# Vision-tower attention: even slots of 100 maxima, two blocks ahead, and 17 bursts of two column-tiled groups per half in place of 25 of one or two

## The chip, the cores and the metric

The kernel runs on one core of a Trainium2 chip. The metric is the device time of one execution in microseconds (us). All four compute engines are used: TensorE (PE in the profile), VectorE (DVE), ScalarE (ACT) and GpSimd (POOL); SyncE (SP) issues nearly all DMAs.

## The reference

```python
h = _L0_tok_ref(x, ...)                                   # windows of 4x4, 8 heads, on 4 images of 56x56x256
h = h + _L0_attn_ref(_layernorm(h), qkv_w, qkv_b, proj_w, proj_b, rpb_table)
h = h + _L0_ffn_ref(_layernorm(h), ...)                   # half of the tokens by a gate, up, gelu, down

def _L0_attn_ref(x, qkv_w, qkv_b, proj_w, proj_b, rpb_table):
    qkv = (x @ qkv_w + qkv_b).reshape(Bw, Nw, 3, nh, dh)  # Bw = 4 images, Nw = 3136 tokens, nh = 8, dh = 32
    q, k, v = (qkv[:, :, 0], qkv[:, :, 1], qkv[:, :, 2])
    attn = jnp.einsum('bnhd,bmhd->bhnm', q * scale, k)
    bias = jnp.transpose(rpb_table[rel_idx], (2, 0, 1))
    attn = jax.nn.softmax(attn + bias[None], axis=-1)
    out = jnp.einsum('bhnm,bmhd->bnhd', attn, v).reshape(Bw, Nw, Cd)
    return out @ proj_w + proj_b
```

The change touches only the middle one, the full attention over the 3136 tokens of each image; its projection is made in a later stage.

## The kernel before, in words

Four stages follow each other: `setup_tables`, `windows_and_qkv`, `full_attention`, `gated_ffn`. Only `full_attention` (from L865) is changed.

**Tiles.** The work is cut into 8 phases (4 images, 2 groups of 4 heads), each phase into 7 halves of `CH` = 448 queries: 56 halves in all. Keys are cut into `KT` = 25 tiles, the first of 64 keys, the others of 128. A half makes 100 scores, one for each key tile and head (`score`, L1130): a product of 97 rows, keys on the output's partitions, 448 queries along it, into one of three banks of `ps_s`. The 97 rows are three stacked parts of 32 (high and low parts of key and query) and a row of ones against a row of shifts. ScalarE takes the exponential of each score from PSUM into `prob`, which has `SLOTS` = 5 places of one key tile and four heads (L1264 to L1279); before it writes place t it waits for the `weigh` and the sum that read the tile five before.

**Shifts and fills.** Softmax needs a shift for each query, its greatest score. It is found a half ahead: for the next half's blocks of `BLK` = 128 queries TensorE makes the products with queries on the partitions (`fill`, L1173), for 4 heads and 7 pieces of 448 keys each, into one of `MB` = 3 banks of `ps_m`; VectorE reduces each to a maximum (`take`, L1288, L1302), reduces the seven of a block for two heads to a negative shift (L1307), TensorE transposes the shifts of four blocks (a "turn", L1184), VectorE copies them (L1297) and SyncE moves them into row 96 of the query tile (`shifts`, L1026). A fill may start only when the reduce of the entry three before it is done (L1179). `max_entries` (L835) lists a phase's 714 entries, 700 maxima and 14 turns, in order, and cuts them into seven slots by `SPILLS`, of 108, 98, 102, 98, 102, 98 and 108 entries; slot s+1 is worked on during half s. The 7 groups of blocks have 4, 3, 4, 3, 4, 3 and 4 blocks. The first block of a group is read from the end of the query tile of the half before, which is `AHEAD` = 5 blocks wide; the others from the group's own tile. The last half has no entries.

**Order on TensorE** (`half`, L1225). After each of the 100 scores come as many entries as keep step with their number, which with 102 is one, and two after scores 49 and 99, and then the burst of that place, if there is one. A burst holds one or two column-tiled groups. A group is four products of 128 rows and 32 output columns, one for each head and each into its own 32 partitions, of 448 queries, in full fp32; each is two instructions, so a group is eight. `weigh` (L1149) multiplies one key tile's `prob` by the values into `ps_o`; `total` (L1161) sums over the partitions, either `prob` of the first tile or one of eight sums over several key tiles that GpSimd adds up (`SUM_TILES`, L1111), into `ps_d`. 25 weighs and 9 totals make 34 groups a half. `weigh` of tile t stands after score 4(t+1)+3, `total` k with the one of them that is 15 scores behind its last tile's first score (L1212 to L1223). So there are 25 bursts, every fourth score, nine of them of two groups. Weigh 24 and totals 7 and 8 fall into the next half.

**Order on VectorE** (`half`, L1326). It takes the entries in their order; before entry `KEEP_AT` = 4 it copies `ps_o` of the half before (`keep_out`, waits for its last weigh), and before entries at 28, 36, ... 84 hundredths of the slot it makes one of 8 reciprocals of `den` (L1320).

**ScalarE** copies `ps_d` to `den` after tile 3 (`keep_den`, L1259). **GpSimd** makes 16 additions a half and one product out x den (`normalize`, L1096), after the addition of tile 21. **SyncE** issues in this order each half: queries of the next half, part of the next phase's keys, the first pair's shift rows, the store of the half before (waits for `normalize`), the second pair's shift rows (L1037 to L1055).

Of the kernel before, what the change touches and what calls it, by code (L numbers as in the profile page):

```python
# [6 lines left out]
ALU = mybir.AluOpType  # L7
ACT = mybir.ActivationFunctionType
AX = mybir.AxisListType
F32 = mybir.dt.float32  # L10
# [9 lines left out]
N = SIDE * SIDE  # L20
NH = 8
DH = C // NH
# [802 lines left out]
AHEAD = 5 * BLK  # L825
# [4 lines left out]
SPILLS = [10, 22, 10, 22, 10, 22, 16]  # L830
# [4 lines left out]
def max_entries():  # L835

    entries, ends = [], []
    for s, blocks in enumerate(GROUP_BLOCKS):
        entries += [("max", s, blocks[0], j, c) for j in range(HG) for c in range(PER_IMAGE)]
        for p in range(2):
            entries += [("max", s, r, j, c) for r in blocks[1:] for j in (2 * p, 2 * p + 1) for c in range(PER_IMAGE)]
            entries.append(("turn", s, p))
    for e in [e for e in entries if e[0] == "turn"]:
        at = entries.index(e)  # L850
        entries.remove(e)
        entries.insert(min(len(entries), at + TURN_AFTER), e)
    maxes, need = 0, [MAX_EACH * (blocks[-1] + 1) + spill for blocks, spill in zip(GROUP_BLOCKS, SPILLS)]
    need[-1] -= SPILLS[-1]
    for n, e in enumerate(entries):
        maxes += e[0] == "max"
        if maxes == need[len(ends)] and (n + 1 == len(entries) or entries[n + 1][0] == "max"):
            ends.append(n + 1)
    begins = [SPILLS[-1]] + ends[:-1]
    slots = [[(e, 0) for e in range(a, z)] for a, z in zip(begins, ends)]  # L860
    slots[-1] += [(e, 1) for e in range(SPILLS[-1])]
    return entries, slots


def full_attention(nc, d):  # L865

    with ExitStack() as ctx:
# [15 lines left out]
        ident = sb("ident3", [128, 128])  # L883
# [107 lines left out]
        def _(sp):  # L991
# [23 lines left out]
            def load_ahead(x):  # L1015

                for row, part in ((0, 0), (DH, 0), (2 * DH, 1)):
                    sp.dma_start(queries[1 - x.v][row:row + DH, :, 4 * BLK:5 * BLK].bitcast(F32),
                                 d.q[x.g, part, :, bass.ds(x.b * N, BLK)].rearrange("(j d) n -> d j n", j=HG)
                                 ).then_inc(ahead_in, 16)  # L1020
# [5 lines left out]
            def shifts(x, p):  # L1026

                sp.wait_ge(m_used, ONE + ENTRIES * x.p + entry_of_turn(x.s, p) + 1)
                for j in range(2):
                    sp.dma_start(queries[x.v][STACK:STACK + 1, 2 * p + j, 0:4 * BLK].bitcast(F32),  # L1030
                                 shift_rows[p][j:8:2, :].bitcast(F32)).then_inc(shift_in[p], 16)
# [51 lines left out]
        def _(pool):  # L1083
            nc.gpsimd.memset(ident[:, :], 0.0).then_inc(id_zero, 1)
            pool.wait_ge(id_zero, ONE + 1)
            nc.gpsimd.affine_select(out=ident[:, :], in_=ident[:, :], compare_op=ALU.not_equal, fill=1.0, base=0,
                                    pattern=[[-1, 128]], channel_multiplier=1).then_inc(id_set, 1)
            pool.wait_ge(id_set, ONE + 1)
            nc.gpsimd.tensor_copy(ident_r[:, :], ident[:, :]).then_inc(idr_set, 1)
# [37 lines left out]
        def _(pe):  # L1127
# [45 lines left out]
            def fill(y, e, next_phase):  # L1173
# [6 lines left out]
                if kind == "turn":  # L1180
                    pair, = what
                    pe.wait_ge(shift_ready, ONE + 2 * PER_IMAGE * p + 2 * group + pair + 1)
                    base = TILE_BLOCK[group]
                    nc.tensor.transpose(ps_m[0:8, e % MB, 0:BLK],  # L1184
                                        shift[:, pair, base:base + 4, :].rearrange("q b j -> q (b j)"),
                                        ident[:, :]).then_inc(m_ready, 1)
                    return
# [3 lines left out]
                ahead = r == GROUP_BLOCKS[group][0] and not very_first  # L1191
# [4 lines left out]
                if j % 2 == 0 and c == 0 and r == (0 if very_first else GROUP_BLOCKS[group][1]):  # L1196
                    pe.wait_ge(q_in[v][j // 2], ONE + 24 * (y.h - y.v) + 48)
                tile = queries[1 - v if ahead else v]
                at = 4 * BLK if ahead else BLK * (r - TILE_BLOCK[group])
# [11 lines left out]

            bursts = {i: [] for i in range(TILES)}  # L1212
            for t in range(KT):
                i = HG * (t + 1) + 3
                bursts[i % TILES].append((weigh, t, i >= TILES))
            bursts[HG * 4 + 3].append((total, 0, False))
            for k, tiles in enumerate(SUM_TILES):
                i = HG * tiles[-1] + 15
                while not bursts[i % TILES]:
                    i += 1  # L1220
                bursts[i % TILES].append((total, k + 1, i >= TILES))
            for i in bursts:
                bursts[i].sort(key=lambda item: not item[2])  # L1223
# [27 lines left out]
            weigh(end, KT - 1)  # L1251
            for i in range(TILES):
                for what, k, of_before in bursts[i]:
                    if of_before and what is total:
                        total(end, k)

        @block.scalar
        def _(act):
# [5 lines left out]
            def half(x):  # L1264
                for t in range(KT):
# [14 lines left out]
                    if t == 3 and x.has_before:  # L1280
                        keep_den(x.h - 1)
# [5 lines left out]
        def _(dve):  # L1287
# [35 lines left out]
            KEEP_AT = 4  # L1323
# [738 lines left out]
```

## Time and profile before

| | us |
|---|---|
| median of 3 runs | 6077.67 |
| lowest, highest | 6074.65, 6080.56 |
| the profiled execution's own time | 6058.31 |
| its span, first to last instruction | 6056.4 |
| PE busy | 5790.5 |
| POOL busy | 4386.0 |
| DVE busy | 4380.1 |
| ACT busy | 3273.6 |

The profile is of one execution. A matmul's row begins when it or its weight load begins, and its end is modelled, so matmuls overlap in it: prices on PE are read from start to start. PEld is the weight load; it is the weight load that carries a matmul's waits. A row of the timeline may merge several instructions of one kind (x4): its duration is from the first one's start to the last one's end. Busy times are the union of the intervals.

### The profile page before, as it was taken

The page shows a single profiled execution, that of the slowest core. Times are in us where ns is not written, and L with a number is a line of the kernel's source. Part 1 is how long each engine was busy: PE and PEld are TensorE (multiplying, and loading weights), DVE is VectorE, ACT ScalarE, POOL GpSimd, SP SyncE. Part 2 cuts the span into 40 slices and gives each one's busy share as a digit, 9 for nine tenths or more (in the row PEclk, how much of TensorE's full clock was granted, in tenths as well). Part 3 has the DMA queues.
Part 4 walks back from the last instruction along what each step waited for, and adds up shares of the span by engine and source line. Part 5 has one row for each costly group of instructions (what it writes and reads, how often), then busy time and mean ns, then how long its engine had stood idle before and what let it go on. Part 6 is the DMA issues. An engine that isn't in the chain of part 4 may idle for free. (4 is left out here: it accounts for less than half of the span.)

```text
span 6056.4 us, 121185 instructions
## 1 busy us (share of the span) xinstructions
PE 5790.5 (96%) x37698; PEld 3429.1 (57%) x37698; DVE 4380.1 (72%) x8484; ACT 3273.6 (54%) x6740; POOL 4386.0 (72%) x1475
## 2 busy tenths in 40 slices
PE   5999998999999999999999999999999999984899
PEld 4777776555555555555555555555555555533566
DVE  4777776777877777777777777777777777736540
ACT  3555454266666666666666666666666666652222
POOL 2444444588888888888888888888888888875453
PEclk9999999799999999999999999999999999997899
DMA  2323223211011111101101110111111000015442
GB/s 73 100 93 105 95 98 112 62 35 37 16 37 33 28 25 37 36 17 37 33 27 25 37 36 17 37 33 27 25 37 36 16 17 17 15 31 160 119 98 44
DMA packets 197572, 297.79 MB, mean 49 GB/s; under 512 B 38038, under 2 KB 162334, under 8 KB 193998
## 3 DMA queue, kind: packets, MB, share of 16 engines
q1 hardware_dynamic: 181958, 269.42, 15.8%
q0 software_dynamic: 12432, 19.38, 1.6%
q8 instruction: 274, 4.49, 0.3%
q10 hardware_dynamic: 2680, 2.63, 0.1%
q14 instruction: 228, 1.87, 0.1%
HBM read 167.63 MB, written 124.50 MB: 48 GB/s over the span
## 5 line engine op out<-in xcount | busy, mean ns | idle before, releaser
L1302 DVE TENSOR_REDUCE tops<-ps_m 128x1 f32<-128x448 f32 (+1 forms) x5600 | 3116.7, 616 | 899.3 <-PE ps_m L1205 863.5
L1278 ACT ACTIVATE prob<-ps_s 128x448 f32<-128x448 f32 (+1 forms) x5600 | 2613.1, 548 | 1739.3 <-PE ps_s L1141 1696.8
L1111 POOL TENSOR_TENSOR tile_sum<-prob 128x1792 f32<-128x1792 f32 x448 | 1803.2, 4025 | 647.2 <-ACT prob L1278 646.8
L1141 PE MATMUL ps_s<-queries,keys 97*128 97x448 f32 (+1 forms) x5600 | 2197.3, 397 | 12.5 <-ACT prob L1278 7.6
L1205 PE MATMUL ps_m<-keys,queries 96*128 96x448 f32 (+1 forms) x5600 | 2090.1, 380 | 28.1 <-DMA keys<-k_parts 25.6
L1111 POOL TENSOR_TENSOR tile_sum<-tile_sum,prob 128x1792 f32<-128x1792 f32 x448 | 1808.0, 4036 | 31.8
L1141 PEld LDWEIGHTS ps_s<-queries,keys 97*128 97x128 f32 (+1 forms) x5600 | 1041.4, 187 | 1152.9 <-ACT prob L1278 661.4
L1157 PE MATMUL ps_o<-prob,values 128*32 128x448 f32 x11200 | 1341.8, 551 | 3.0 <-ACT prob L1278 1.2
L1205 PEld LDWEIGHTS ps_m<-keys,queries 96*128 96x128 f32 (+1 forms) x5600 | 1061.2, 190 | 234.1 <-DVE tops L1302 89.5
L1157 PEld LDWEIGHTS ps_o<-prob,values 128*32 128x32 f32 x11200 | 226.5, 108 | 379.4 <-issue 245.0
L1169 PE MATMUL ps_d<-tile_sum,ones 128*32 128x448 f32 x3584 | 420.9, 541 | 3.3 <-POOL tile_sum L1111 3.3
L331 POOL TENSOR_TENSOR logit<-logit,top 112x896 f32<-112x896 f32 x112 | 190.5, 1701 | 237.3 <-DVE top L602 237.3
L612 DVE RECIPROCAL rden<-sums 128x224 f32<-128x224 f32 x112 | 173.6, 1550 | 123.9 <-ACT sums L751 123.9
L391 PE MATMUL ps_q<-xT,w_qkv 128*128 128x224 f32 x896 | 203.2, 371 | 50.7 <-DMA bias_proj<-in_b_proj 50.7
L1169 PEld LDWEIGHTS ps_d<-tile_sum,ones 128*32 128x32 f32 x3584 | 110.7, 110 | 211.4 <-issue 206.5
L1320 DVE RECIPROCAL den<-den 128x56 f32<-128x56 f32 x448 | 217.5, 488 | 14.5 <-ACT den L1262 14.5
L342 POOL TENSOR_TENSOR lo<-full,hi 128x448 fp32r<-128x448 f32 x112 | 127.2, 1136 | 116.8 <-DVE hi L658 116.8
L337 POOL TENSOR_TENSOR rstd<-veps,minus_half 112x4 f32<-112x4 f32 x28 | 33.8, 1208 | 240.2 <-DVE veps L647 240.2
L391 PEld LDWEIGHTS ps_q<-xT,w_qkv 128*128 128x128 f32 x896 | 163.6, 193 | 63.4 <-DMA bias_proj<-in_b_proj 50.7
L1712 PE MATMUL ps_h<-xT,w_up 128*128 128x512 f32 (+1 forms) x416 | 179.9, 584 | 0.9 <-ACT xT L1776 0.7
L1722 PE MATMUL ps_y<-w_down,hT 128*128 128x256 f32 x784 | 177.1, 381 | 0.0
L739 ACT ACTIVATE prob<-logit 112x896 f32<-112x896 f32 x112 | 106.0, 947 | 123.5 <-POOL logit L331 123.4
(181 smaller groups left out, 4096.3 us busy)
## 6 DMA issues: line engine op xcount, KB each, us to landing
queries<-q_parts SPq DMA_DIRECT2D x288, 160.0 KB, 3.3
keys<-k_parts SPq DMA_DIRECT2D x96, 392.0 KB, 7.1
xT<-in_x SPq DMA_DIRECT2D x56, 224.0 KB, 2.6
hidden_and_bias<-base SPq DMA_DIRECT2D x28, 448.0 KB, 3.1
q_parts<-hi SPq DMA_DIRECT2D x56, 224.0 KB, 1.9
q_parts<-lo SPq DMA_DIRECT2D x56, 224.0 KB, 1.9
k_parts<-hi SPq DMA_DIRECT2D x56, 224.0 KB, 1.9
k_parts<-lo SPq DMA_DIRECT2D x56, 224.0 KB, 1.9
```

The lines of the kernel that those rows point to most:

```text
L331: nc.gpsimd.tensor_tensor(logit[p][:, :, :], logit[p][:, :, :], top[p][:, :].unsqueeze(2).broadcast_to([GROUP, NH, GROUP]), ALU.subtract). ...
L391: mm = nc.tensor.matmul(ps_q[:, bank, k * UNIT:(k + 1) * UNIT], w[:, c, job * 128:(job + 1) * 128], xT[u][:, c, :], start=(c == 0), stop=( ...
L1111: nc.gpsimd.tensor_tensor(tile_sum[k % 2][:, :, :], left, prob[:, t % SLOTS, :, :], ALU.add).then_inc(summed, 1)
L1141: mm = nc.tensor.matmul(o[:, 0:CH], keys[x.u][:, j, at:at + k], queries[x.v][:, j, own:own + CH], start=True, stop=not last, skip_group_ch ...
L1157: mm = nc.tensor.matmul(ps_o[j * DH:(j + 1) * DH, 0:CH], values[x.u][:, t, j * DH:(j + 1) * DH], prob[:, t % SLOTS, j, :], start=(t == 0), ...
L1169: mm = nc.tensor.matmul(ps_d[j * DH:(j + 1) * DH, 0:CH], ones[:, int(k > 0), :], moving, start=(k == 0), stop=(k == SUMS))
L1205: mm = nc.tensor.matmul(o[:, 0:CH], tile[0:STACK, j, at:at + rows], keys[u][0:STACK, j, c * CH:(c + 1) * CH], start=True, stop=not corner, ...
L1278: nc.scalar.activation(prob[0:k, t % SLOTS, j, :], ps_s[0:k, score_bank(x.hm, i), 0:CH], ACT.Exp).then_inc(exp_done, 1)
L1302: nc.vector.tensor_reduce(tops[0:rows, j, r - blocks[0], c:c + 1], ps_m[0:rows, e % MB, 0:CH], AX.X, ALU.max).then_inc(m_used, 1)
L1320: nc.vector.reciprocal(den[:, piece * w:(piece + 1) * w], den[:, piece * w:(piece + 1) * w]).then_inc(recip_done, 1)
L1712: mm = nc.tensor.matmul(ps_h[:, t % 2, 0:w], w_up[:, c, t * 128:(t + 1) * 128], xT[:, c, 0:w], start=(c == 0), stop=(c == CT - 1))
L1722: mm = nc.tensor.matmul(ps_y[:, r // 2, (r % 2) * C:(r % 2 + 1) * C], hT[:, t, r * ROWS:(r + 1) * ROWS], w_down[:, t, :], start=(t == 0), ...
```

## The change

- A group's first two blocks (`MORE` = 2), no longer one, are read from the tile of the half before, so the query tiles are 6 blocks wide (`OWN` + `MORE`) and `load_ahead` brings two blocks.
- `SPILLS` are such that every slot has 100 maxima and 2 turns.
- The bursts are written out: 17 a half, after scores 3, 11, 16, 21, 26, 31, and then every sixth to 97, each of two groups; eight of them hold two weighs, nine a weigh and a total. Weigh 0 stands after score 16 (7 before), total 0 too (19 before); weigh 24 after score 11 of the next half (3 before).
- `KEEP_AT` is 12, and ScalarE's `keep_den` comes after score 13, no longer after score 15.
- The fp32 identity is built in `out[0]` and not kept; the turns use the rounded one.

```diff
--- before.py
+++ after.py
@@ -822,12 +822,13 @@
 
 
 BLK = 128
-AHEAD = 5 * BLK
+OWN, MORE = 4, 2
+AHEAD = (OWN + MORE) * BLK
 PHASES = B * G
 GROUP_BLOCKS = [range(-(-7 * s // 2), -(-7 * (s + 1) // 2)) for s in range(PER_IMAGE)]
 TILE_BLOCK = [7 * s // 2 for s in range(PER_IMAGE)]
 MAX_EACH = HG * PER_IMAGE
-SPILLS = [10, 22, 10, 22, 10, 22, 16]
+SPILLS = [8, 24, 12, 28, 16, 32, 20]
 TURN_AFTER = 3
 SUM_TILES = [(1, 2, 3, 4)] + [(t, t + 1, t + 2) for t in range(5, 23, 3)] + [(23, 24)]
 
@@ -842,9 +843,9 @@
 
     entries, ends = [], []
     for s, blocks in enumerate(GROUP_BLOCKS):
-        entries += [("max", s, blocks[0], j, c) for j in range(HG) for c in range(PER_IMAGE)]
+        entries += [("max", s, r, j, c) for r in blocks[:MORE] for j in range(HG) for c in range(PER_IMAGE)]
         for p in range(2):
-            entries += [("max", s, r, j, c) for r in blocks[1:] for j in (2 * p, 2 * p + 1) for c in range(PER_IMAGE)]
+            entries += [("max", s, r, j, c) for r in blocks[MORE:] for j in (2 * p, 2 * p + 1) for c in range(PER_IMAGE)]
             entries.append(("turn", s, p))
     for e in [e for e in entries if e[0] == "turn"]:
         at = entries.index(e)
@@ -880,7 +881,6 @@
         corner_lo = sb("corner_lo3", [128, HG, BLK], F32R)
         prob = sb("prob3", [128, SLOTS, HG, CH])
         tile_sum = [sb(f"tile_sum{i}", [128, HG, CH]) for i in range(2)]
-        ident = sb("ident3", [128, 128])
         ident_r = sb("ident_r", [128, 128], F32R)
         ones = sb("ones3", [128, 2, DH])
         tops = sb("tops", [BLK, HG, 4, PER_IMAGE])
@@ -1015,8 +1015,8 @@
             def load_ahead(x):
 
                 for row, part in ((0, 0), (DH, 0), (2 * DH, 1)):
-                    sp.dma_start(queries[1 - x.v][row:row + DH, :, 4 * BLK:5 * BLK].bitcast(F32),
-                                 d.q[x.g, part, :, bass.ds(x.b * N, BLK)].rearrange("(j d) n -> d j n", j=HG)
+                    sp.dma_start(queries[1 - x.v][row:row + DH, :, OWN * BLK:AHEAD].bitcast(F32),
+                                 d.q[x.g, part, :, bass.ds(x.b * N, MORE * BLK)].rearrange("(j d) n -> d j n", j=HG)
                                  ).then_inc(ahead_in, 16)
 
             def load_corner(x):
@@ -1027,7 +1027,7 @@
 
                 sp.wait_ge(m_used, ONE + ENTRIES * x.p + entry_of_turn(x.s, p) + 1)
                 for j in range(2):
-                    sp.dma_start(queries[x.v][STACK:STACK + 1, 2 * p + j, 0:4 * BLK].bitcast(F32),
+                    sp.dma_start(queries[x.v][STACK:STACK + 1, 2 * p + j, 0:OWN * BLK].bitcast(F32),
                                  shift_rows[p][j:8:2, :].bitcast(F32)).then_inc(shift_in[p], 16)
 
             def store(x):
@@ -1081,12 +1081,12 @@
 
         @block.gpsimd
         def _(pool):
-            nc.gpsimd.memset(ident[:, :], 0.0).then_inc(id_zero, 1)
+            nc.gpsimd.memset(out[0][:, 0:128], 0.0).then_inc(id_zero, 1)
             pool.wait_ge(id_zero, ONE + 1)
-            nc.gpsimd.affine_select(out=ident[:, :], in_=ident[:, :], compare_op=ALU.not_equal, fill=1.0, base=0,
-                                    pattern=[[-1, 128]], channel_multiplier=1).then_inc(id_set, 1)
+            nc.gpsimd.affine_select(out=out[0][:, 0:128], in_=out[0][:, 0:128], compare_op=ALU.not_equal, fill=1.0,
+                                    base=0, pattern=[[-1, 128]], channel_multiplier=1).then_inc(id_set, 1)
             pool.wait_ge(id_set, ONE + 1)
-            nc.gpsimd.tensor_copy(ident_r[:, :], ident[:, :]).then_inc(idr_set, 1)
+            nc.gpsimd.tensor_copy(ident_r[:, :], out[0][:, 0:128]).then_inc(idr_set, 1)
             pool.wait_ge(idr_set, ONE + 1)
             nc.gpsimd.memset(ones[:, 1, :], 1.0).then_inc(rows_set, 1)
             for u in range(2):
@@ -1183,20 +1183,20 @@
                     base = TILE_BLOCK[group]
                     nc.tensor.transpose(ps_m[0:8, e % MB, 0:BLK],
                                         shift[:, pair, base:base + 4, :].rearrange("q b j -> q (b j)"),
-                                        ident[:, :]).then_inc(m_ready, 1)
+                                        ident_r[:, :].bitcast(F32)).then_inc(m_ready, 1)
                     return
                 r, j, c = what
                 u, v = (y.u + next_phase) % 2, (y.v + group + PER_IMAGE * next_phase - y.s) % 2
                 very_first = isinstance(p, int) and p == 0 and group == 0
-                ahead = r == GROUP_BLOCKS[group][0] and not very_first
+                ahead = r in GROUP_BLOCKS[group][:MORE] and not very_first
                 if group == 0 and r == 0 and c == 0:
                     pe.wait_ge(k_in[u][j], ONE + 48 * (y.b + int(next_phase and y.g == 1) + 1))
                     if j == 0 and not very_first:
                         pe.wait_ge(ahead_in, ONE + 48 * p)
-                if j % 2 == 0 and c == 0 and r == (0 if very_first else GROUP_BLOCKS[group][1]):
+                if j % 2 == 0 and c == 0 and r == (0 if very_first else GROUP_BLOCKS[group][MORE]):
                     pe.wait_ge(q_in[v][j // 2], ONE + 24 * (y.h - y.v) + 48)
                 tile = queries[1 - v if ahead else v]
-                at = 4 * BLK if ahead else BLK * (r - TILE_BLOCK[group])
+                at = BLK * (OWN + r - GROUP_BLOCKS[group][0] if ahead else r - TILE_BLOCK[group])
                 rows = min(BLK, N - BLK * r)
                 corner = r == 0 and c == PER_IMAGE - 1
                 if corner and j == 0:
@@ -1209,18 +1209,22 @@
                                           start=False, stop=True, skip_group_check=True)
                 mm.then_inc(m_ready, 1)
 
+
             bursts = {i: [] for i in range(TILES)}
-            for t in range(KT):
-                i = HG * (t + 1) + 3
-                bursts[i % TILES].append((weigh, t, i >= TILES))
-            bursts[HG * 4 + 3].append((total, 0, False))
-            for k, tiles in enumerate(SUM_TILES):
-                i = HG * tiles[-1] + 15
-                while not bursts[i % TILES]:
-                    i += 1
-                bursts[i % TILES].append((total, k + 1, i >= TILES))
-            for i in bursts:
-                bursts[i].sort(key=lambda item: not item[2])
+
+            def burst(i, *groups):
+                bursts[i % TILES] += [(what, k, i >= TILES) for what, k in groups]
+
+            burst(16, (weigh, 0), (total, 0))
+            burst(21, (weigh, 1), (weigh, 2))
+            burst(26, (weigh, 3), (weigh, 4))
+            for k, tiles in enumerate(SUM_TILES[:6]):
+                i, t = HG * tiles[-1] + 15, 5 + 3 * k
+                burst(i, (total, k + 1), (weigh, t))
+                burst(i + 6, (weigh, t + 1), (weigh, t + 2))
+            burst(TILES + 3, (total, 7), (weigh, 23))
+            burst(TILES + 11, (weigh, 24), (total, 8))
+            assert len(SUM_TILES) == 8 and KT == 25
 
             def half(x):
                 y = after(x)
@@ -1248,11 +1252,10 @@
             pe.wait_ge(rows_set, ONE + 3)
             halves(pe, half)
             end = Half(FIRST_ROUND, HALVES - 1)
-            weigh(end, KT - 1)
             for i in range(TILES):
                 for what, k, of_before in bursts[i]:
-                    if of_before and what is total:
-                        total(end, k)
+                    if of_before:
+                        what(end, k)
 
         @block.scalar
         def _(act):
@@ -1277,8 +1280,8 @@
                         act.wait_ge(s_ready, ONE + x.h * TILES + i + 1)
                         nc.scalar.activation(prob[0:k, t % SLOTS, j, :], ps_s[0:k, score_bank(x.hm, i), 0:CH],
                                              ACT.Exp).then_inc(exp_done, 1)
-                    if t == 3 and x.has_before:
-                        keep_den(x.h - 1)
+                        if t == 3 and j == 1 and x.has_before:
+                            keep_den(x.h - 1)
 
             halves(act, half)
             keep_den(HALVES - 1)
@@ -1320,7 +1323,7 @@
                 nc.vector.reciprocal(den[:, piece * w:(piece + 1) * w],
                                      den[:, piece * w:(piece + 1) * w]).then_inc(recip_done, 1)
 
-            KEEP_AT = 4
+            KEEP_AT = 12
             RECIP_SCORES = [2 * HG * (k + 3) + HG for k in range(RECIPS)]
 
             def half(x):
```

## Rows read from the trace of the kernel before

**Rows 1.** The page: engines' busy time, and the granted clock in 40 slices

```profile
PE 5790.5 (96%) x37698; PEld 3429.1 (57%) x37698; DVE 4380.1 (72%) x8484; ACT 3273.6 (54%) x6740; POOL 4386.0 (72%) x1475
...
PEclk9999999799999999999999999999999999997899
```

**Rows 2.** Windows, the attention stage: stretch, us, busy (count) by engine, clock, DMA

```profile
core 0: us, PE busy (x) PEld busy (x) DVE busy (x) ACT busy (x) POOL busy (x), PEclk, DMA share, GB/s
1140.12:5426.80 4286.68, 4260.91 (x26513) 2320.57 (x26511) 3298.22 (x6196) 2637.06 (x5655) 3668.39 (x951) 1.00 0.11 28
```

**Rows 3.** Windows with the maxima (L1205) alone: four halves, one phase

```profile
2131.94:2211.02 79.08, 39.74 (x106) 20.05 (x106) 1.00 0.06 17
...
1750.91:1826.92 76.01, 36.86 (x100) 18.94 (x100) 1.00 0.16 41
1826.92:1901.65 74.73, 35.31 (x96) 18.17 (x96) 1.00 0.14 33
...
2052.49:2131.94 79.45, 39.01 (x106) 18.55 (x106) 1.00 0.06 16
...
1675.12:2211.02 535.90, 258.64 (x700) 131.02 (x700) 1.00 0.12 30
```

**Rows 4.** Waits from 1400 to 5000 us: total us, times, longest

```profile
PEld ps_m L1205 <- DVE tops L1302: 55.8, 209, 0.4
```

**Rows 5.** Timeline of PE from 2057 us: start us, us, instruction

```profile
2057.78 0.96 PE L1157 MATMUL ps_o<-prob,values 128*32 128x448 f32 x8
2058.67 0.47 PE L1141 MATMUL ps_s<-queries,keys 97*128 97x448 f32 x1
2058.98 0.37 PE L1205 MATMUL ps_m<-keys,queries 96*128 96x448 f32 x1
...
2060.22 0.37 PE L1205 MATMUL ps_m<-keys,queries 96*128 96x448 f32 x1
2060.51 0.96 PE L1169 MATMUL ps_d<-tile_sum,ones 128*32 128x448 f32 x8
...
2062.16 0.47 PE L1141 MATMUL ps_s<-queries,keys 97*128 97x448 f32 x1
```

**Rows 6.** Timeline of all engines from 2061 us

```profile
2062.47 0.58 PE L1205 MATMUL ps_m<-keys,queries 96*128 96x448 f32 x2
...
2062.88 2.75 DVE L1302 TENSOR_REDUCE tops<-ps_m 128x1 f32<-128x448 f32 x5 [1.27 <-PE ps_m L1205]
...
2063.55 0.19 PEld L1205 LDWEIGHTS ps_m<-keys,queries 96*128 96x128 f32 x1 [0.27 <-DVE tops L1302]
...
2063.86 0.36 PE L1141 MATMUL ps_s<-queries,keys 97*128 97x448 f32 x1
...
2064.49 0.96 PE L1157 MATMUL ps_o<-prob,values 128*32 128x448 f32 x8
```

**Rows 7.** Timeline of all engines from 2173 us: a reciprocal between reduces

```profile
2172.65 1.15 DVE L1302 TENSOR_REDUCE tops<-ps_m 128x1 f32<-128x448 f32 x2
...
2173.72 0.49 DVE L1320 RECIPROCAL den<-den 128x56 f32<-128x56 f32 x1
...
2174.12 0.56 DVE L1302 TENSOR_REDUCE tops<-ps_m 128x1 f32<-128x448 f32 x1
...
2174.60 0.26 DVE L1297 CAST shift_rows<-ps_m 8x128 fp32r<-8x128 f32 x1
```

**Rows 8.** Timelines of POOL, SP and PE at a half's end

```profile
2434.65 1.17 POOL L1098 TENSOR_TENSOR out<-out,den 128x448 f32<-128x448 f32 x1
...
2435.99 0.38 SPq L1035 DMA_DIRECT2D attention_out<-out  x1
2436.48 1.23 SPq L1030 DMA_DIRECT2D queries<-shift_rows  x2
...
2439.93 0.42 PE L1141 MATMUL ps_s<-queries,keys 97*64 97x448 f32 x1
```

## The prediction

> **What bounds the kernel now.** I read the page first: TensorE is busy 96% of the span, and its granted clock has the digit 9 in nearly every slice [rows 1]. Then the windows: the attention stage, from its first score to its last group, is 4287 us of the 6056, with PE busy 4261, DVE 3298, ACT 2637, POOL 3668, clock 1.00, the 2.4 GHz level [rows 2]. Per half (56 of them) that is 76.5 us long, DVE 58.9, ACT 47.1, POOL 65.5. So PE sets the pace, and the change touches only this stage.
>
> Next the halves: one with 98 entries (96 maxima in the row, two turns) takes 74.7 us, with 102 entries 76.0, with 108 entries 79.1 and 79.5; a whole phase of seven takes 535.9 [rows 3]. Four entries more cost 1.3 us, but the next six cost 3.2: beyond 102 something else than streaming is paid. The waits name it: the weight load of a maximum waits 55.8 us in 209 cases for DVE's reduce, because ps_m has three banks [rows 4].
>
> The PE timeline gives the prices [rows 5]. Score and maximum alternate 0.207 us apart (2058.98 to 2060.22 is six steps). From a burst's first matmul to the next score a burst of one group takes 0.89, of two 1.64: a group streams 0.75. A run of four pairs and a burst of one is 2060.51 - 57.78 = 2.73 us; less 8 x 0.207 and 0.75, **0.33 us is the fixed price of going to column tiles and back**. Check: a half with 98 entries has 25 x 0.33 + 34 x 0.75 = 33.75, plus 198 x 0.207 = 41.0, together 74.7, as the row says. It has no stall. By the same sum 102 entries give 75.6 and 108 give 76.8: stalls of 0.4, and of 2.3 and 2.6. A phase before has two halves of 102 and two of 108: 5.8 us of stall.
>
> **Step 1, bursts.** 34 groups stay (25 weigh, 9 total); 25 switches become 17. Over 56 halves 8 x 0.33 x 56 = **-148 us**. Eight of the new bursts hold two weighs, one bank for both, which no row shows. Bounds: 1.64 us as with ps_d beside it, or 2 x 0.89 = 1.78 if the second had to begin afresh, which would cost up to 8 x 56 x 0.14 = 63 us; below 1.64 nothing is to be had, as 0.75 per group is streaming. I take 1.64: within a group both passes of a head already go to one bank, and a group into ps_o and one into ps_d last 0.96 alike [rows 5].
>
> **Step 2, even slots.** The entries stay 714 a phase, so PE streams the same; every half gets 102. The 108-entry halves' stalls go. I take all the old stalls out here and put all new ones in below: 7 phases x 5.8 and 0.9 in the last (which has no following phase to fill for) = **-42 us**.
>
> **Step 3, the longer runs between bursts.** This is the step that decides. In a run PE delivers a maximum each 0.414 us, DVE takes 0.53: five reduces in 2.75 us, four steps after one of 0.61 [rows 6]. Three banks and the burst, during which DVE catches up, hide that while a run has four maxima. The run of rows 6 has five, two of them back to back, and shows the rule. First maximum at 2062.47, its reduce 2062.88 (+0.41) to 2063.49; the fourth maximum's weight load starts 2063.55, the next score at 2063.86, so the fourth really began streaming 0.21 before that, 2063.65: 0.16 after the reduce's end. So with F0 = 0, the maximum k may not stream before 0.41 + 0.61 + 0.53 (k - 3) + 0.16 = 1.18 + 0.53 (k - 3). Unhindered it comes at 0.414 k. The excess of the last maximum is the run's stall: five maxima 1.71 - 1.66 = 0.05; six 2.24 - 2.07 = 0.17; eight 3.30 - 2.90 = 0.40; seven in six score steps (two back to back) 2.77 - 2.28 = 0.49. Applied to rows 6 (the fifth at 1.71 instead of 1.45) it gives 0.26; the run lasts 2064.49 - 62.16 = 2.33 against 1.84 and 0.21 for the extra entry, so 0.28.
>
> The new bursts stand after scores 3, 11, 16, 21, 26, 31, then every sixth to 97. One run of eight pairs (4 to 11): 0.40. Four of five pairs: 0.20. From 98 over the border to 3, six scores with seven entries, as each half's hundredth score carries two: 0.49. Eleven of six pairs, of which that of 44 to 49 has seven entries: 10 x 0.17 + 0.49 = 2.2. Sum 3.3.
>
> On top come the reciprocals. One back to back with reduces costs DVE 0.41 (2173.72 to 2174.12) [rows 7]. They are put before entries 28, 36, 44, 53, 61, 69, 77, 85. Those at a run's first entry (44, 69) fall into the burst; those at its fifth or later (36, 61, 85) delay no release that the run still needs; 28 (second of 27 to 31), 53 and 77 (third of six) delay the last release by 0.41 each: 1.2. Together 4.5 us a half; the turns (a small reduce more, but a cast of 0.26 [rows 7] for a reduce of 0.61) about cancel. 55 halves carry entries: 55 x 4.5 = **+248 us**. In the old order runs had four maxima, and a reciprocal delayed only releases behind the next burst. KEEP_AT 12 puts the copy of ps_o (0.6 us) before the first reduce behind burst 11; weigh 24 leads that burst and its 0.96 and the copy end within the 1.64 and the 0.7 until DVE is wanted: nothing.
>
> **Step 4, what else moves.** Weighs come later (0 at 16 instead of 7, 24 at 111 instead of 103), so ScalarE's five prob slots could run short. Tile t needs weigh t-5: tile 5 begins at score 20, weigh 0 is at 16; tile 11 at 44, weigh 6 at 37; always at least three scores of room. keep_den after score 13 has burst 11 before it, and total 0 stands behind weigh 0 in burst 16: 2.1 + 0.75 us for two exponentials and a copy: nothing. POOL needs 65.5 us a half, 12 under the new one, and no total moves nearer its sum than in the old order. Two blocks ahead make the query loads 768 columns wide; DMA is at 0.11 [rows 2], and the first entry that needs the new tile comes at entry 24 to 48 of a half instead of 6: hidden. On SP the shift rows of the second pair are queued behind the store, which waits for POOL's normalize: ends 2435.82, store issued 2435.99, shifts 2436.48 to 2437.71, while the score that needs them comes in the half that begins 2439.93 (the row with 64 keys), at its third [rows 8]. With two bursts instead of four in that stretch (1.5 us less) this room shrinks but stays: nothing, 56 us if not. The prologue does two entries less: -1. The spare identity is gone, no time.
>
> **The sum.** -148 - 42 + 248 - 1 = +57 us against the profiled execution's 6058.3 (span 6056.4): 6115. The median of the runs is 19 above it, so I forecast 6077.7 + 57 = 6135 us, with halves of 41.8 + 31.1 + 4.5 = 77.4 us, all nearly alike.
>
> The trace shows DVE with 77% of the stage [rows 2], so by busy time alone it binds nothing; it binds inside a run. The Trainium skill (TensorEngine Tiling (Array Packing), PSUM Bottleneck) warns that once tiling has sped TensorE up, the copy out of PSUM may become the limit. Taken as a rule for the average, DVE's 59 us a half would lie far below PE's 73 and the change would win; this case's waits [rows 4] side with the warning, but per run.
>
> **Rivals.** *Not slower:* DVE keeps up in the long runs, say because the reduce of the burst's leftover is always done and releases come earlier than the 0.16 that I read from one run. It is decided at (148 + 42 + 1) / 55 = 3.5 us of stall a half; below that the gains win. With no more stall than now (0.7) the time is 6078 - 191 + 39 = 5926; with releases earlier by 0.05 and reciprocals harmless it is 4.5 - 0.7 - 1.2 = 2.6 a half, 6030. For it: DVE is idle a quarter of the time. Against: rows 3, where six entries more cost 3.2 us instead of 1.2. Chance 0.09. *Slower by more:* the shift rows arrive 1 us late in every half, behind normalize and store on SP, 6135 + 56 = 6191; or two weighs in a burst cost 1.78, 6198. For it: 1.5 us less room, no row of such a burst. Against: 2 us are free now. Chance 0.08. *No change,* within 0.2%, about what a measurement of this kernel can tell from none: 12 us either way: stalls of 3.3 to 3.7, chance 0.03.
>
> **How the numbers follow.** My case has 0.80. Its bounds: stalls 3.9 to 5.1 a half, from the release known to 0.03 us (twelve runs) and one reciprocal more or less: 33 us either way, 6102 to 6168. To hold 8 in 10 I reach a little towards the rivals, 6098 to 6173. Faster 0.08, same 0.03, slower 0.89.
>
> **What would show it.** 17 fixed prices a half; PE's weight load for ps_m waiting for DVE not 55.8 us but several times that, in nearly every run; runs of six pairs at 2.9 us and of five at 2.3, those with a reciprocal at the places named 0.4 longer; halves within 0.6 us of each other near 77.4. I am wrong if the halves are under 76.5, if waits for shift_rows or ps_o appear, or if a burst of two weighs isn't 1.64.

## The result, and the profile after

The changed kernel takes 6136.6 us (median of 4, 6134.1 to 6137.7) against 6076.2 us (6074.0 to 6080.6): 1.0099 times as long, 95% interval 1.0087 to 1.0112. Forecast: 6135.

The profiled executions differ by 76 us, not 60: 6134.1 against 6058.3. The attention stage accounts for 4347.3 - 4286.7 = 60.6 [rows 2]; most of the rest lies behind it, in code that the change does not touch (642 us from the stage's last group to the end, against 630). Below, kernels are compared by medians beside runs of the kernel before of the same series (it took 6076.7 us in one series and 6063.4 in another on the same chip), or by the attention stage in their profiles: behind it the eleven profiles show 628 to 649 us, and two profiles of one kernel, the even slots with the old bursts, 649 and 629. Windows of the changed kernel, first the stage, then three halves with the busy times of the maxima alone:

```profile
core 0: us, PE busy (x) PEld busy (x) DVE busy (x) ACT busy (x) POOL busy (x), PEclk, DMA share, GB/s
1142.77:5490.10 4347.33, 4290.41 (x26515) 2324.30 (x26513) 3236.53 (x6198) 2605.10 (x5655) 3663.44 (x951) 1.00 0.12 30
...
1760.76:1838.13 77.37, 39.42 (x101) 18.85 (x100) 1.00 0.17 42
1838.13:1915.66 77.53, 39.68 (x101) 18.85 (x100) 1.00 0.15 35
2147.54:2225.39 77.85, 39.57 (x101) 18.84 (x100) 1.00 0.08 19
```

Beside [rows 3]: every half has its 100 maxima, and where the halves took 74.7, 76.0 and 79, they now take 77.2 to 77.9. The first of a phase, which has the corner products, takes 78.3, and four halves at two loop ends 80 to 82 (last section). The waits from 1400 to 5000 us:

```profile
DVE tops L1305 <- PE ps_m L1205: 841.3, 766, 3.4
PEld ps_m L1205 <- DVE tops L1305: 358.8, 1403, 2.1
```

The second answers to [rows 4]: 358.8 us in 1403 waits for 55.8 in 209. And DVE waits for PE more than twice that, 841.3 us. Neither engine is late all the time; each waits for the other at different moments. The timeline of the changed kernel shows it in a run of six pairs (entries 32 to 37), ahead of a burst of two weighs:

```profile
1786.35 0.47 PE L1141 MATMUL ps_s<-queries,keys 97*128 97x448 f32 x1
...
1786.66 0.37 PE L1205 MATMUL ps_m<-keys,queries 96*128 96x448 f32 x1
...
1787.07 2.22 DVE L1305 TENSOR_REDUCE tops<-ps_m 128x1 f32<-128x448 f32 x4 [1.23 <-PE ps_m L1205]
...
1788.28 0.19 PEld L1205 LDWEIGHTS ps_m<-keys,queries 96*128 96x128 f32 x1 [0.18 <-DVE tops L1305]
...
1788.81 0.19 PEld L1205 LDWEIGHTS ps_m<-keys,queries 96*128 96x128 f32 x1 [0.23 <-DVE tops L1305]
...
1789.21 0.49 DVE L1323 RECIPROCAL den<-den 128x56 f32<-128x56 f32 x1
1789.21 1.71 PE L1157 MATMUL ps_o<-prob,values 128*32 128x448 f32 x16
...
1790.86 0.47 PE L1141 MATMUL ps_s<-queries,keys 97*128 97x448 f32 x1
```

DVE has idled 1.23 us, begins 0.41 after the first maximum, and at the fifth and sixth PE's weight load waits for a bank. The run lasts 1789.21 - 1786.35 = 2.86 us. The burst of two weighs then lasts 1.65, like the 1.64 of a weigh and a total [rows 5]; of the changed kernel's bursts with maxima around them, 931 of 934 last 1.64. Here the reciprocal (for entry 36) comes late in the run and costs it nothing. The run of entries 51 to 56, whose reciprocal stands before its third entry (timelines of PE and DVE):

```profile
1800.39 0.47 PE L1141 MATMUL ps_s<-queries,keys 97*128 97x448 f32 x1
...
1803.20 0.47 PE L1205 MATMUL ps_m<-keys,queries 96*128 96x448 f32 x1 [0.20 <-DVE tops L1305]
1803.60 0.96 PE L1169 MATMUL ps_d<-tile_sum,ones 128*32 128x448 f32 x8
...
1801.10 1.15 DVE L1305 TENSOR_REDUCE tops<-ps_m 128x1 f32<-128x448 f32 x2 [1.22 <-PE ps_m L1205]
1802.17 0.49 DVE L1323 RECIPROCAL den<-den 128x56 f32<-128x56 f32 x1
1802.59 2.14 DVE L1305 TENSOR_REDUCE tops<-ps_m 128x1 f32<-128x448 f32 x4
```

It lasts 3.21 us, 0.35 more.

### The profile page after: what moved, and what is told of

The parts are those of the page before. It is cut to its first block and busy times, and to the rows that moved or that the text cites. A ratio compares the mean times of both kernels' runs of the same rounds, so it can differ in the third digit from the quotient of the medians.

```text
span 6132.3 us, 121188 instructions
## 1 busy us (share of the span) xinstructions
PE 5822.9 (95%) x37698; PEld 3433.1 (56%) x37698; DVE 4316.3 (70%) x8484; ACT 3241.5 (53%) x6740; POOL 4381.3 (71%) x1475
## 5 line engine op out<-in xcount | busy, mean ns | idle before, releaser
L1305 DVE TENSOR_REDUCE tops<-ps_m 128x1 f32<-128x448 f32 x5600 | 3079.6, 611 | 1033.4 <-PE ps_m L1205 1023.6
L1205 PE MATMUL ps_m<-keys,queries 96*128 96x448 f32 x5600 | 2228.6, 403 | 64.7 <-DVE tops L1305 33.3
L1141 PE MATMUL ps_s<-queries,keys 97*128 97x448 f32 (+1 forms) x5600 | 2162.6, 389 | 9.3 <-ACT prob L1281 4.1
L1205 PEld LDWEIGHTS ps_m<-keys,queries 96*128 96x128 f32 x5600 | 1055.8, 189 | 568.1 <-DVE tops L1305 442.7
L1157 PE MATMUL ps_o<-prob,values 128*32 128x448 f32 x11200 | 1242.4, 545 | 0.9 <-DVE out L1317 0.9
L1157 PEld LDWEIGHTS ps_o<-prob,values 128*32 128x32 f32 x11200 | 307.0, 109 | 537.5 <-issue 351.9
L1629 POOL DMA_INDIRECT out<-out,xs x49 | 77.2, 1575 | 135.1 <-DVE out L1967 125.3
```

Source lines behind the costliest of these rows:

```text
L1141: mm = nc.tensor.matmul(o[:, 0:CH], keys[x.u][:, j, at:at + k], queries[x.v][:, j, own:own + CH], start=True, stop=not last, skip_group_ch ...
L1157: mm = nc.tensor.matmul(ps_o[j * DH:(j + 1) * DH, 0:CH], values[x.u][:, t, j * DH:(j + 1) * DH], prob[:, t % SLOTS, j, :], start=(t == 0), ...
L1205: mm = nc.tensor.matmul(o[:, 0:CH], tile[0:STACK, j, at:at + rows], keys[u][0:STACK, j, c * CH:(c + 1) * CH], start=True, stop=not corner, ...
L1305: nc.vector.tensor_reduce(tops[0:rows, j, r - blocks[0], c:c + 1], ps_m[0:rows, e % MB, 0:CH], AX.X, ALU.max).then_inc(m_used, 1)
```

## The experiments

**The even slots alone.** The changed kernel with the bursts of before:

```diff
-            burst(16, (weigh, 0), (total, 0))
...
-            burst(TILES + 11, (weigh, 24), (total, 8))
+            for t in range(KT):
+                i = HG * (t + 1) + 3
+                bursts[i % TILES].append((weigh, t, i >= TILES))
...
-                        if t == 3 and j == 1 and x.has_before:
-                            keep_den(x.h - 1)
+                    if t == 3 and x.has_before:
+                        keep_den(x.h - 1)
...
-            KEEP_AT = 12
+            KEEP_AT = 4
```

> The even slots and two blocks ahead alone, with the 25 bursts, KEEP_AT and keep_den of before. My theory (the excess over streaming is PE waiting in long runs for DVE to free one of three ps_m banks): only the stalls of the 108-entry halves go, all full halves take 76.0 to 76.2 us, a phase 534 instead of 536, the whole about 16 us less than before (6060). Rival (even slots bring a cost of their own: wider query loads, the last turn of a half coming later): waits for shift_rows or queries appear and the time is at or above before.

6056.6 us beside 6076.7, ratio 0.9964 (0.9950 to 0.9977): 20 us less, and the stage is 4268.2, 18.5 less. Full halves take 75.8 to 76.2, the first of a phase 76.5, a phase 532.2 for 535.9. So evening out the slots is a gain by itself, and the loss of the change is in its bursts.

**The new bursts alone**, on the old slots:

```diff
-OWN, MORE = 4, 2
+OWN, MORE = 4, 1
-SPILLS = [8, 24, 12, 28, 16, 32, 20]
+SPILLS = [10, 22, 10, 22, 10, 22, 16]
```

> The 17 bursts (with KEEP_AT 12 and the earlier keep_den) on the old slots of 98 to 108 entries. My theory: 8 x 0.33 us a half are saved, and the runs of five, six and eight pairs stall more: halves with 98 entries near 76.0 (74.8 before), with 102 near 77.0 (76.0), with 108 between 80.5 and 82.5 (79.1 and 79.4); the whole about 70 us over before, 6147. Rival (the stalls have nothing to do with how many entries a run holds, but a burst of two weighs costs 1.78 instead of 1.64): all halves longer by the same amount, those of 108 under 80.

6152.5 us, ratio 1.0127 (1.0112 to 1.0143): 76 us more. Windows with the maxima alone, halves of 98, 108, 108, 98 (this one with the corner products) and 102 entries:

```profile
2541.99:2617.97 75.98, 37.88 (x97) 18.10 (x96) 1.00 0.15 38
2617.97:2700.12 82.15, 41.45 (x107) 18.46 (x106) 1.00 0.05 15
2700.12:2780.70 80.58, 42.41 (x107) 19.95 (x106) 1.00 0.06 16
2780.70:2857.41 76.71, 37.88 (x97) 18.11 (x96) 1.00 0.14 33
2857.41:2934.11 76.70, 39.23 (x101) 18.85 (x100) 1.00 0.16 40
```

Beside [rows 3], a half of 98 is 1.2 us longer, one of 102 by 0.7, and the two of 108 by 2.7 and 1.5. A higher price of a burst would be the same in every half, and both halves of 108 would lie under 80: the rival falls. But the loss does not simply grow with the entries; between 98 and 102 it shrinks. Where DVE's other work falls counts as well. In the halves of 98 the copy of ps_o comes after the first entry of a run of five and not before it, and the run lasts 2.85 us, not 2.33. And the 2.7 holds a wait of another kind, a turn (last row) whose shift is not ready, with a reciprocal among the reduces just before it on DVE; before, no turn waited so long:

```profile
2552.17 0.61 DVE L1317 COPY out<-ps_o 128x448 f32<-128x448 f32 x1
...
2553.36 0.47 PE L1205 MATMUL ps_m<-keys,queries 96*128 96x448 f32 x1 [0.34 <-DVE tops L1305]
...
2687.36 0.27 PE L1184 MATMUL ps_m<-ident_r,shift 128*8 128x128 f32 x1 [1.58 <-DVE shift L1310]
```

**Reciprocals ahead of the runs.**

```diff
-                pieces = [scores * len(slot) // TILES for scores in RECIP_SCORES]
+                pieces = [27, 32, 38, 44, 51, 57, 63, 69] if slot else [0] * RECIPS
```

> The changed kernel with its eight reciprocals put before the first entry behind a burst (entries 27, 32, 38, 44, 51, 57, 63, 69) instead of 28, 36, 44, 53, 61, 69, 77, 85. My theory: the three that delay a bank inside a run cost 0.41 us each, so a half takes 76.0 to 76.6 and the whole 66 us less than the changed kernel, 6070. Rival (reciprocals are harmless, as DVE idles a quarter of the time): 6137 as it is.

6083.6 us beside 6076.7 (ratio 1.0009, 1.0000 to 1.0018), where the changed kernel took 6136.6 beside 6076.2. Moving eight small instructions on an engine that idles a quarter of the time brings 53 us, where I had expected 66; by the halves (76.2 to 76.8 for 77.2 to 77.9) it is 1.0 to 1.1 each. The rival falls; the price was 0.35 per reciprocal, not 0.41, which over three reciprocals and 55 halves is 58 us and not 68. PE's waits for ps_m sink only to 312.6 us in 1401: what is left are the small waits of every run. They are enough: even so, 17 bursts on even slots are no faster than the kernel before.

**Shorter reduces.** The changed kernel, and the kernel before, with VectorE reducing 224 of each 448 keys, and so leaving half of the scores out of the maxima:

```diff
-                nc.vector.tensor_reduce(tops[0:rows, j, r - blocks[0], c:c + 1], ps_m[0:rows, e % MB, 0:CH],
+                nc.vector.tensor_reduce(tops[0:rows, j, r - blocks[0], c:c + 1], ps_m[0:rows, e % MB, 0:CH // 2],
```

> The changed kernel with each of VectorE's reduces reading only the first 224 of the 448 keys: half of the scores are left out of the maxima, everything on the other engines stays. My theory: DVE then is never behind, PE's waits for ps_m vanish, halves fall from 77.3-78.3 to 73.0-73.3 us and the whole to about 5887. Rival (the lost time is in the bursts or in what ScalarE and GpSimd release): little changes, still above 6076.

> The kernel before with the same shortened reduces (half of the keys left out of the maxima). My theory: only its few stalls go, about 35 to 42 us: 6037, halves of 74.8, 75.6 and 76.9 by their number of entries. The run of the changed kernel with the same reduces then lies 148 us below this one, the price of eight switches into column tiles and back in each of 56 halves, 0.33 us each. Rival (the switches are cheaper in pairs only, or two weighs in one burst cost 0.14 more): a difference under 90 us.

5864.8 and 6016.7 us, beside 6063.4 in their series: 0.9675 (0.9659 to 0.9692) and 0.9923 (0.9907 to 0.9940). Windows of the changed kernel with the edit, the stage and two halves:

```profile
1130.05:5234.11 4104.06, 4087.76 (x26515) 2386.32 (x26513) 2293.54 (x6198) 2582.82 (x5655) 3669.71 (x951) 1.00 0.13 32
...
1713.47:1786.18 72.71, 36.44 (x101) 19.00 (x100) 1.00 0.18 45
1786.18:1858.91 72.73, 36.44 (x101) 19.01 (x100) 1.00 0.16 37
```

its wait of PE for ps_m:

```profile
PEld ps_m L1205 <- DVE tops L1305: 4.2, 9, 1.6
```

and of the kernel before with the same edit, the stage and a half of 102 and of 98 entries:

```profile
1130.57:5381.80 4251.23, 4231.23 (x26513) 2322.57 (x26511) 2368.52 (x6196) 2630.60 (x5655) 3669.15 (x951) 1.00 0.11 28
...
1736.13:1811.65 75.52, 36.57 (x100) 19.02 (x100) 1.00 0.16 41
1811.65:1886.40 74.75, 35.41 (x96) 18.26 (x96) 1.00 0.14 34
```

This is the clearest pair. DVE's reduces take 243 us of the changed kernel's stage (4347.3 - 4104.1) and 35 of the other's (4286.7 - 4251.2), though nothing but DVE's pace was changed. With them out of the way the change is worth 6016.7 - 5864.8 = 152 us. The stages alone differ by 4251.2 - 4104.1 = 147.2, and the loop ends cost the changed kernel 5 us more there, so eight switches fewer in each of 56 halves bring 152, or 0.34 each. A half of 98 entries stays at 74.75: it had no stall. (Both also start the stage 10 to 13 us sooner: before it, DVE finds the first shifts.)

**Twenty bursts.** Even slots, a burst after every fifth score, 14 of two groups and 6 of one, reciprocals at runs' first entries (the lines of the 17 bursts go):

```diff
...
+            burst(9, (weigh, 0))
+            burst(19, (total, 0), (weigh, 2))
+            burst(24, (weigh, 3), (weigh, 4))
+            for i, t in ((29, 5), (39, 7), (54, 11), (74, 16), (89, 20)):
+                burst(i, (weigh, t))
+            for k, (i, t) in enumerate(((34, 6), (44, 8), (59, 12), (69, 15), (79, 17), (94, 21))):
+                burst(i, (total, k + 1), (weigh, t))
+            for i, t in ((49, 9), (64, 13), (84, 18), (99, 22)):
+                burst(i, (weigh, t), (weigh, t + 1))
+            burst(TILES + 4, (weigh, 24), (total, 7))
+            burst(TILES + 14, (total, 8))
+            burst(14, (weigh, 1))
...
-                        if t == 3 and j == 1 and x.has_before:
-                            keep_den(x.h - 1)
+                    if t == 3 and x.has_before:
+                        keep_den(x.h - 1)
...
-            KEEP_AT = 12
+            KEEP_AT = 5
...
+                pieces = [30, 35, 40, 45, 51, 56, 61, 66] if slot else [0] * RECIPS
```

> Even slots with 20 bursts, after every fifth score (14 of two groups, 6 of one), reciprocals at the first entry behind a burst. My theory: a run of five pairs stalls 0.05 us and one of six 0.17, so 20 x 0.33 and small stalls are less than 25 x 0.33 with few and 17 x 0.33 with many: halves of 75.6 to 76.2, the whole near 6040, faster than both kernels. Rival (what costs time is that weighs and totals come later or in pairs, not the length of runs): not under 6076.

6052.7 us beside 6076.7, ratio 0.9962 (0.9948 to 0.9975): faster than both, but 13 us over what I expected and no better than the even slots alone. Runs of five pairs take 2.33 us (2.87 with a sixth entry, twice a half), except one of each half, with 2.58. The timeline shows which:

```profile
1762.43 0.47 PE L1141 MATMUL ps_s<-queries,keys 97*128 97x448 f32 x1
...
1763.38 0.54 ACT L1268 ACTIVATE den<-ps_d 128x448 f32<-128x448 f32 x1
...
1763.80 1.86 ACT L1284 ACTIVATE prob<-ps_s 128x448 f32<-128x448 f32 x4
...
1764.40 0.19 PEld L1141 LDWEIGHTS ps_s<-queries,keys 97*128 97x128 f32 x1 [0.39 <-ACT prob L1284]
```

keep_den stands behind the run's first exponential and delays the release of a bank of ps_s: the same mechanism, on the other engine.

**keep_den one score earlier** than in the twenty bursts, so that it falls into burst 14:

```diff
-                    if t == 3 and x.has_before:
-                        keep_den(x.h - 1)
+                        if t == 3 and j == 2 and x.has_before:
+                            keep_den(x.h - 1)
```

> The twenty bursts with ScalarE's keep_den after score 14, inside burst 14, instead of after score 15. In the run without this the run of five pairs after burst 14 lasts 2.58 us where the others last 2.33. My theory: there the score after next waits for an exponential that stands behind keep_den; moved, the run falls to 2.33, which is 0.25 x 55 = 14 us: near 6039 on a chip where before takes 6077. Rival (the run is long for another reason, a reduce or the copy of ps_o): it stays 2.58 and the time within 3 us.

**The same with the reciprocals inside the runs:**

```diff
-                pieces = [30, 35, 40, 45, 51, 56, 61, 66] if slot else [0] * RECIPS
+                pieces = [scores * len(slot) // TILES for scores in RECIP_SCORES]
```

> The same with the reciprocals back at entries 28, 36, 44, 53, 61, 69, 77, 85. In runs of five pairs that is the fourth, second, fifth, third, first of 61, fourth, second and fifth entry; only those at the second entry (36, 77) or inside the run of six entries (53 isn't) can delay a bank that the run still needs. My theory: two of them cost 0.41 us each and a half gains 0.4 to 1.0 us, 20 to 50 us in all over the one with reciprocals behind bursts. Rival (harmless): the same time.

**And the even slots again**, beside them:

> The kernel with even slots and the old 25 bursts again, to have it on the same chip as the twenty bursts. By phases of 532.2 us (even slots) against 532.6 less 7 x 0.25 = 530.9 (twenty bursts, keep_den earlier) I expect it 10 us slower than those.

Beside 6060.6 of the kernel before on this chip: 6030.8 (0.9946, 0.9932 to 0.9959), 6061.6 (1.0000, 0.9991 to 1.0009) and 6043.6 (0.9970, 0.9958 to 0.9982). The stage and two halves of the first:

```profile
1142.61:5396.78 4254.17, 4230.60 (x26515) 2352.74 (x26513) 3273.63 (x6198) 2604.33 (x5655) 3663.86 (x951) 1.00 0.12 31
...
1749.45:1825.28 75.83, 38.51 (x100) 18.92 (x100) 1.00 0.18 44
1825.28:1900.91 75.63, 38.37 (x100) 18.91 (x100) 1.00 0.15 36
```

The long run is gone (2.33), and the stage is 4266.1 - 4254.2 = 12 us shorter than before that edit, where I had put 14. By medians the gain over the kernel before of the same series goes from 24.0 to 29.8 us; this step of 6 is too little to be told from none. With 20 bursts and the two clean-ups this is the best version: 30 us under the kernel before, 13 under the even slots alone, and this pair, not the run before, shows that 20 bursts gain something by themselves. Putting the reciprocals back inside costs 31 us, which takes it back to the time of the kernel before: in most halves two runs with a reciprocal before their second entry take 2.69 and not 2.33, 0.35 each, where I had put 0.41.

## Why the prediction was right

- **The switch's 0.33 us** [rows 5] gave -148; the pair with short reduces measures -147 by the stages and -152 without the loop ends, 0.34 each.
- **Two weighs in one burst** were taken at 1.64, the price of a weigh and a total; they take that, and the 63 us of the rival did not come.
- **The even slots** were taken at -42, all stalls of before; the short reduces take 35 off the stage. By themselves they bring 17 to 20, since two entries back to back still stall a little, twice in every half (a run of four pairs with a fifth entry lasts 2.32 us, where 1.85 and 0.21 would be 2.06).
- **The long runs** were the deciding term: 4.5 us a half, +248. With short reduces 243 go from the stage. The lengths that the chain of reads and releases gave, 2.3 for five pairs, 2.9 for six, 0.40 of excess for eight, 0.49 for seven entries, are seen: runs of 2.33 and 2.86 us, of 3.92 for eight pairs (from 1764.54 us; 0.31 to the first maximum, 3.30 to the last, 0.29 to the burst: 3.90) and of 3.39 for seven entries (from 1795.36; by the same sum 3.37).
- **The reciprocals** at 28, 53 and 77 were put at 0.41 each; they cost 0.34 to 0.36, and moving them brings 1.0 to 1.1 us a half where I had put 1.2. The others are harmless, as said: that at 36 costs nothing in the timeline above.
- **What I costed at nothing** (later weighs, GpSimd, wider query loads, the shift rows behind the store) shows no wait.
- **Halves** of 77.4, within 0.6 us: 77.2 to 77.9, but the phase's first, with its corner products, 78.3, and the loop ends' 80 to 82, for which the stated spread of 0.6 us left no room.
- **Not foreseen, and luck:** the changed kernel loses some 3 us more at each of two loop ends (last section). Both stall terms were put 5 to 7 us too large (-42 for -35, +248 for +243), with opposite signs, so that in the total they nearly cancel. The sum of 57 is 3 to 4 us short of the measured 60.4 (medians) and 60.6 (stages). That 6135 lies within 2 us of 6136.6 is luck to that extent: the median it was added to, 6077.7 of three runs, is 6076.2 with the fourth.

The prediction cites the Trainium skill (TensorEngine Tiling (Array Packing), PSUM Bottleneck) for the warning that the copy out of PSUM may become the limit. It was right here in this form: not by busy time, where DVE has 74% of the stage after the change, but inside a run, where three banks cannot bridge 0.53 us against 0.41. The products that wait are the maxima's, which are not column-tiled themselves.

## What to carry to other kernels

A consumer with a quarter of its time idle still holds the producer up, if the work comes in runs longer than the banks between them bridge: write the two paces and the release of the bank down as a chain along one run, and count what each further item costs, before trading fewer switches for longer runs. Place small extra work of the consumer (a reciprocal, a copy) in the gaps between runs and never ahead of a release that the run still needs. The optimum lies where one more saved switch (here 0.33 us) costs as much in stalls. Of the three orders tried on even slots, that with five pairs a run was the fastest, not that with four and not that with mostly six and one of eight; others were not tried.

## What the runs showed of the hardware that was not expected

The kernel's loop over images comes round twice, after halves 14 and 28 (counted from 0), and there both kernels lose time, the changed one more: the two halves around the first end take 80.0 + 81.4 us where their like take 78.3 + 77.4, so 5.7 too many, against 77.8 + 76.4 in place of 75.8 + 76.0, 2.3, before; at the second end it is 6.0 against 3.4. DVE's slower pace is not the reason, as with short reduces it is 6.2 and 6.1 against 3.7 and 3.5. The changed kernel's timelines of PE and DVE at the first end:

```profile
2305.41 0.42 PE L1141 MATMUL ps_s<-queries,keys 97*64 97x448 f32 x1 [1.53 <-issue]
...
2308.27 2.22 DVE L1305 TENSOR_REDUCE tops<-ps_m 128x1 f32<-128x448 f32 x4 [3.40 <-issue]
...
2308.95 0.74 PE L1205 MATMUL ps_m<-keys,queries 96*128 96x448 f32 x1 [1.47 <-DVE tops L1305]
2309.62 1.72 PE L1169 MATMUL ps_d<-tile_sum,ones 128*32 128x448 f32 x8
2311.11 1.72 PE L1157 MATMUL ps_o<-prob,values 128*32 128x448 f32 x8
```

and windows over PE's first wait, the time in which DVE is late, and the slow groups, with the clock and the DMA share ahead of the last column:

```profile
2303.90:2305.40 1.50, 0.00 (x0) 0.00 (x0) 0.97 (x2) 0.10 (x1) 1.32 (x1) 1.00 0.05 16
2305.40:2308.30 2.90, 2.06 (x7) 1.07 (x7) 0.03 (x1) 1.82 (x4) 2.67 (x1) 0.76 0.77 194
2308.50:2313.50 5.00, 4.55 (x19) 1.58 (x20) 1.99 (x4) 0.00 (x0) 0.00 (x0) 0.50 0.99 240
```

PE's first instruction of the new round is 1.53 us late and DVE's 3.40, with nothing in the profile that they wait for. PE, which had idled 1.53 us, has its granted clock at 0.50, the 1.2 GHz level, from 2306.92 to 2313.75, and idles another 1.47 in that time: a group takes 1.49 us from start to start and not 0.75.

The kernel before, where PE idled once at each end, shows both outcomes. At the first end, after 1.95 us, the clock stayed at 1.00. At the second it fell, after a shorter idle:

```profile
3362.82 0.41 PE L1141 MATMUL ps_s<-queries,keys 97*64 97x448 f32 x1 [1.78 <-issue]
...
3363.31:3366.72 3.41, 3.41 (x15) 1.76 (x17) 2.50 (x4) 2.04 (x4) 1.22 (x1) 0.50 0.98 257
```

So the idle's length alone does not tell here whether the clock falls, and that end costs 3.4 us and not 2.3. What the instructions are late for was not tried. The DMA engines are 0.05 busy while PE waits in the changed kernel, so busy DMA engines do not explain that wait. In the 2.9 us in which DVE is late they are 0.77 busy, with the next half's queries, and no run shows whether the two are connected.
